# A graph-transformer layer on one core: the routing to the experts rebuilt, and weights split earlier

## The reference, cut to what matters

```python
xn = _layernorm(x)                                # x: 1250 x 1024, float32
x = x + gnn(xn, W, a, src, dst) + mix(xn, w_query_left, w_query_right, w_key, w_value)
x = x + ffn(_layernorm(x), gate_W, gate_b, expert_W, expert_b)

# gnn: h = xn @ W; e = exp(-leaky_relu(al[src] + ar[dst])) over 20000 edges;
#      elu(segment_sum(e * h[dst], src) / (segment_sum(e, src) + 1e-5))
# mix: ((xn @ w_ql) * (xn @ w_qr)) @ ((xn @ w_key).T @ (xn @ w_value))
# ffn: scores = maximum(x @ gate_W + gate_b, 1e-4); p = softmax(scores)      # 8 experts
#      the two largest of p are chosen; w = maximum(p, 0.1) / (sum of the chosen two)
#      out = sum over the chosen experts e of (x @ expert_W[e] + expert_b[e]) * w[e] / 2
```

## Time and profile before

| | us |
|---|---|
| median of 3 runs (1270.72 to 1272.55) | 1272.45 |
| the profiled execution, its own time | 1271.35 |
| its span | 1269.5 |
| PE busy in the span | 1190.3 (94%) |
| DVE busy | 760.4 (60%) |
| POOL busy | 486.7 (38%) |
| ACT busy | 305.9 (24%) |

### The profile page before, as it was taken

The page is one execution under the profiler, slowest core; times in us unless marked ns, Lnnn a source line. Parts: engine busy times, 40 slices in busy tenths (PEclk is TensorE's granted clock), DMA queues, the critical chain, the costliest instruction groups (busy, mean ns, idle before and its releaser), DMA issues.

```text
span 1269.5 us, 16268 instructions
## 1 busy us (share of the span) xinstructions
PE 1190.3 (94%) x5807; PEld 1002.7 (79%) x5807; DVE 760.4 (60%) x1525; ACT 305.9 (24%) x412; POOL 486.7 (38%) x446
## 2 busy tenths in 40 slices
PE   6999999999998999999999999899946799999996
PEld 5788888878787989899878878788744688878884
DVE  7979522453423777777663347989557933463544
ACT  2412112222110111211012323333243501331321
POOL 3940677878785000000000017455302444443443
PEclk9999999999998999999999999899957899999998
DMA  5110442834211233211054422333354974694844
GB/s 204 34 34 34 124 111 67 284 112 120 64 43 27 90 98 100 78 54 55 21 148 150 145 81 88 127 126 138 148 191 174 354 228 88 121 350 91 232 102 81
DMA packets 89623, 156.08 MB, mean 123 GB/s; under 512 B 14628, under 2 KB 45086, under 8 KB 89428
## 3 DMA queue, kind: packets, MB, share of 16 engines
q1 hardware_dynamic: 74148, 129.76, 29.7%
q0 software_dynamic: 15408, 25.44, 11.2%
HBM read 112.95 MB, written 42.04 MB: 122 GB/s over the span
## 4 chain that ended last, share of the span: by engine, by line
PE 57%; POOL 18%; DVE 15%; issue 8%; DMA 1%; ACT 1%; DVEq 0%; POOLq 0%; ACTq 0%
PE ps L1548 17%; PE ps L1549 17%; PE ps L1550 17%; POOL tab_d L650 16%; DVE e_lo L1463 3%; PE ps L1676 2%; PE ps L1738 2%; PE ps L1766 1%; DVE xn_lo L1017 1%; DVE stats L991 1%; PE ps L1635 1%; DMA e_raw<-in_L_ffn_expert_W 1%; DVE place_sum L1094 1%; DVE place L1092 1%; DVE place L1091 1%
## 5 line engine op out<-in xcount | busy, mean ns | idle before, releaser
L650 POOL DMA_INDIRECT tab_d<-val_i,addr_i x160 | 206.7, 1292 | 114.7 <-issue 114.7
L1548 PE MATMUL ps<-e_hi,lt_hi 128*128 128x512 f32 x368 | 147.8, 402 | 15.2 <-DVE lt_lo L1468 10.8
L668 POOL TENSOR_TENSOR att_part<-att 128x640 f32<-128x640 f32 x10 | 17.5, 1752 | 358.1 <-PE ps L1550 350.0
L1550 PE MATMUL ps<-e_hi,lt_lo 128*128 128x512 f32 x368 | 144.4, 392 | 0.0
L1549 PE MATMUL ps<-e_lo,lt_hi 128*128 128x512 f32 x368 | 144.2, 392 | 0.0
L1548 PE MATMUL ps<-xt_hi,q_hi 128*128 128x416 f32 (+1 forms) x384 | 143.4, 373 | 0.0
L1549 PE MATMUL ps<-xt_lo,q_hi 128*128 128x416 f32 (+1 forms) x384 | 136.2, 355 | 0.0
L1550 PE MATMUL ps<-xt_hi,q_lo 128*128 128x416 f32 (+1 forms) x384 | 135.7, 353 | 0.0
L1226 DVE TENSOR_TENSOR cnt<-ps,cnt 128x256 f32 x208 | 87.1, 419 | 42.3 <-PE ps L1676 28.1
L761 POOL DMA_INDIRECT out<-y,row_put x46 | 74.8, 1625 | 97.7 <-DVE y L1530 57.5
L1548 PEld LDWEIGHTS ps<-e_hi,lt_hi 128*128 128x128 f32 x368 | 69.6, 189 | 33.9 <-DVE yb L1525 14.6
(11 more groups left out here) (302 smaller groups left out, 2681.7 us busy)
## 6 DMA issues: line engine op xcount, KB each, us to landing
e_raw<-in_L_ffn_expert_W SPq DMA_DIRECT2D x64, 512.0 KB, 6.2
acc<-in_x SPq DMA_DIRECT2D x18, 512.0 KB, 8.9
w_raw<-in_L_mix_w_key SPq DMA_DIRECT2D x16, 512.0 KB
h_d<-hs SPq DMA_DIRECT2D x18, 256.0 KB
q_in<-q_d SPq DMA_DIRECT2D x9, 512.0 KB, 4.9
h_in<-h_d SPq DMA_DIRECT2D x9, 512.0 KB, 5.3
mix_d<-ms SPq DMA_DIRECT2D x18, 256.0 KB
mix_in<-mix_d SPq DMA_DIRECT2D x9, 512.0 KB, 3.2
```

Of the source, the lines that this page charges most:

```text
L650: nc.gpsimd.indirect_dma_start(out=tab_d, out_offset=bass.IndirectOffsetOnAxis(ap=addr_i[0:EP, j:j + 1], axis=0), in_=val_i[0:EP, j:j + 1] ...
L1548: nc.tensor.matmul(o, lh, rh, start=(k == 0), stop=False)
L1550: return nc.tensor.matmul(o, ll, rh, start=False, stop=(k == last_k))
```

## The change

The gaps "..." leave out declarations and index forms that only follow from what is shown.

1. Counting starts one PE job later, and DVE zeroes `cnt` in place of POOL.

```diff
+        TICK_FIRST = 3
         def tick_slots(j):
             per_job = 2
-            return range(min(NTK, per_job * max(0, j - 2)), min(NTK, per_job * max(0, j - 1)))
+            return range(min(NTK, per_job * max(0, j - TICK_FIRST)), min(NTK, per_job * max(0, j + 1 - TICK_FIRST)))
...
-            pool.wait_ge(s_wlo, UNITS * C_END)
-            pool.wait_ge(s_alsum, 1)
-            nc.gpsimd.memset(cnt[...].bitcast(f32), 0.0).then_inc(s_cz, 1)
...
             dve.wait_ge(s_alsum, 1)
+            V.memset(cnt[...].bitcast(f32), 0.0).then_inc(s_cz, 1)
             dve.wait_ge(s_tabr, 16)
```

```diff
+            for t in range(NT):
+                if t == NT - 1:
+                    rows_transposed(NT - 3)
...
+            nodes_half(NT - 1, 0)
+            weight_sums(NT - 1)
+            nodes_half(NT - 1, 1)
+            rows_transposed(NT - 2)
+            gate(NT - 4)
+            gate(NT - 3)
+            gate(NT - 2)
+            rows_transposed(NT - 1)
+            gate(NT - 1)
...
+                    pieces = [(NH - 1, slice(0, D))] if i < NT - 1 else [(h, slice(h * HALF, (h + 1) * HALF)) for h in range(NH)]
```

```diff
+                if t == 4:
+                    sp.wait_ge(s_full, first["GNN"])
+                    load_expert(0, range(MB))
+                if t == NT:
+                    sp.wait_ge(s_full, GNN_END)
+                    load_expert(0, range(MB, KB))
...
+            gate_in(NT - 3)
+            nodes_out(NT - 1)
+            act.wait_ge(s_full, GNN_END)
+            expert_hi(0, range(0, 1))
+            gate_in(NT - 2)
+            expert_hi(0, range(1, FIRST_LO))      # FIRST_LO = 3
+            gate_in(NT - 1)
+            expert_hi(0, range(FIRST_LO, KB))
             act.wait_ge(s_gate, 1)
             nc.scalar.activation(g_p[:, :, :], g_p[:, :, :], ACT.Exp).then_inc(s_gexp, 1)
...
+            expert_hi(1, range(FIRST_LO))
```

```diff
+            V.memset(sc[:, :, :], 0.0)
...
+            expert_lo(0, range(FIRST_LO))
+            dve.wait_ge(s_gate_used, NT)
...
+            V.tensor_reduce(g_tot[:, :], g_in[:, :, :], AX.X, ALU.add).then_inc(s_gtot, 1)
+            V.tensor_tensor(g_p[...], S, over_experts(g_m[:, :]), ALU.subtract).then_inc(s_gate, 1)
+            link(V.tensor_tensor_scan(g_run[...], flat2, flat2, 0.0, ALU.add, ALU.max))
+            link(V.tensor_copy(g_ends[:, 1:NE + 1], g_run[:, :, NT - 1]))
+            link(V.scalar_tensor_tensor(g_run[...], g_run[...], -1.0 - MID, over_ends(g_ends[:, 0:NE]), ALU.add, ALU.subtract))
+            dve.wait_ge(s_gtotp, 1)
+            link(V.tensor_scalar(g_nb[:, :], ps[:, 7, NE:2 * NE], 1.0 / P, MID / P, ALU.mult, ALU.add))
+            link(V.tensor_scalar(g_nb[:, :], g_nb[:, :], ROUND, None, ALU.add))
+            link(V.tensor_scalar(g_nb[:, :], g_nb[:, :], -ROUND, 1.0, ALU.add, ALU.max))
+            link(V.tensor_tensor_scan(g_cum[...], g_nb[...], g_nb[...], 0.0, ALU.add, ALU.max))
+            link(V.tensor_tensor(g_nb[:, :], g_cum[:, :], g_nb[:, :], ALU.subtract))
+            link(V.scalar_tensor_tensor(g_place[...], g_nb[...], float(P), ps[:, 7, 0:NE], ALU.mult, ALU.add))
+            V.tensor_tensor(g_pos[...], ...).then_inc(s_gpos, 1)
...
+            link(V.tensor_tensor(g_prod[:, :, :, :], g_pick[:, :, :, :], g_pos[...], ALU.mult))
+            link(V.tensor_reduce(p_f[:, :, :], g_prod[:, :, :, :], AX.X, ALU.add))
+            link(V.tensor_scalar(p_hi[...], p_f[...], 1.0 / P, ROUND, ALU.mult, ALU.add))
+            link(V.tensor_scalar(p_hi[...], p_hi[...], -ROUND, None, ALU.add))
+            link(V.scalar_tensor_tensor(p_lo[...], p_hi[...], -float(P), p_f[...], ALU.mult, ALU.add))
+            token_rows(0)                          # tok_r of the first choice, 128x1280
+            link(V.tensor_tensor(tok_s[...], ...))  # both choices, 128x580
+            for c in range(2):
+                last = V.tensor_tensor(tok_c[:, c * NT:(c + 1) * NT, :], ...)
+            last.then_inc(s_toks, 1)
+            token_rows(1).then_inc(s_toks, 1)
+            V.tensor_copy(bounds[:, 1:NE + 1], g_cum[:, :])
+            V.scalar_tensor_tensor(pad_0[...], g_nb[...], float(P), ps[:, 7, NE:2 * NE], ALU.mult, ALU.add)
+            dve.wait_ge(s_tokp, 1)
+            V.tensor_scalar(tok_of[:, :], ps[:, 2, 0:NSLOT], -1.0, 0.0, ALU.add, ALU.max).then_inc(s_route, 1)
+            V.tensor_scalar(slot_f[:, :], ps[:, 2, 0:NSLOT], -1.0, None, ALU.add)
```

```diff
-            gather(0)
+            gather_rows(tok_of[:, 0:1])
...
-            expert_lo(0, range(0, 1))
             block_lo(0, 0)
-            expert_lo(0, range(1, MB + 1))
+            expert_lo(0, range(FIRST_LO, MB + 1))
             block_lo(0, 1)
             expert_lo(0, range(MB + 1, KB))
...
+        AHEAD = [4] + [6] * (NE - 2)
             for e in range(NE):
                 if e + 1 < NE:
-                    expert_lo(e + 1)
+                    expert_lo(e + 1, range(AHEAD[e]))      # ACT: expert_hi(e + 1, range(0 if e else FIRST_LO, AHEAD[e]))
                 ... # the blocks of expert e
+                if e + 1 < NE:
+                    expert_lo(e + 1, range(AHEAD[e], KB))  # ACT: expert_hi(e + 1, range(AHEAD[e], KB))
...
                 if e >= 1:
                     sp.wait_ge(s_ye, first_block[e] * 2 + 2)
                     load_bias(e + 1)
+                if e + 2 < NE:
+                    load_expert(e + 2, range(KB), running=e)
```

More of the change, by code:

```diff
@@ L735, in _ @@
[L735 to L740 removed]
+            step(G.tensor_tensor(pad_at[:, :], pad_pre[:, :], pad_0[:, :], ALU.add))
@@ L1371, in _, with expert_lo @@
             dve.wait_ge(s_tri2, 3)
-            link(V.memset(sc[:, :, :], 0.0))
+            def expert_lo(e, rows):
+                for k in rows:
+                    dve.wait_ge(s_ehi, KB * e + k + 1)
+                    V.tensor_tensor(e_lo[e % 2][:, k, :], e_raw[k][:, :], e_hi[e % 2][:, k, :].bitcast(f32),
+                                    ALU.subtract).then_inc(s_elo, 1)
+            g_one, g_two = g_pick[:, 0], g_pick[:, 1]
+            V.memset(sc[:, :, :], 0.0)
+            V.memset(g_ends[:, :], 0.0)
+            V.memset(bounds[:, 0:1], 0)
+            V.tensor_scalar(io_mid[:, :], io16[:, :], -MID, None, ALU.add)
+            link(V.tensor_scalar(valid[:, :], tok[:, :], float(N), None, ALU.is_lt))
+            link(V.scalar_tensor_tensor(tokv[:, :], tok[:, :], 1.0, valid[:, :], ALU.add, ALU.mult))
+            expert_lo(0, range(FIRST_LO))
             dve.wait_ge(s_gate_used, NT)
@@ new lines, in gate @@
+            def gate(i):
+                w = ROWS[i]
+                if i == 0:
+                    pe.wait_ge(s_gw, 32)
+                    pe.wait_ge(s_cadd, NC)
+                pe.wait_ge(*released(tr_job[i] + 1))
+                for k in range(KB):
+                    last = nc.tensor.matmul(ps[0:w, 7, i * NE:(i + 1) * NE], xg[:, i % 2, k, 0:w], gw[:, k, :],
+                                            start=(k == 0), stop=(k == KB - 1))
+                last.then_inc(s_gate_used, 1)
@@ new lines, in rows_transposed, with nodes_half @@
+            def rows_transposed(i):
+                pe.wait_ge(s_xn2, NT + i + 1)
+                for g in range(2):
+                    n = tr_job[i] + g
+                    bank_free(n)
+                    transposes(n, xn2[:, i % 2, :], g, ROWS[i])
+            def nodes_half(t, h):
+                w, n = ROWS[t], gnn_half(t, h)
+                bank_free(n)
+                for d in range(NT):
+                    r = ROWS[d]
+                    last = three(ps[0:w, n % NB, :], att_hi[t % 2][0:r, d, 0:w], att_lo[t % 2][0:r, d, 0:w],
+                                 h_hi[0:r, d, h * HALF:(h + 1) * HALF], h_lo[0:r, d, h * HALF:(h + 1) * HALF], d, NT - 1)
+                last.then_inc(s_full, 1)
@@ new lines, in weight_sums @@
+            def weight_sums(t):
+                w, n = ROWS[t], gnn_sum(t)
+                bank_free(n)
+                pe.wait_ge(s_sum, t + 1)
+                nc.tensor.matmul(ps[0:w, n % NB, 0:2], att_sum[:, t % 2, 0:w], ones[:, 0:2], start=True, stop=True).then_inc(s_full, 1)
+            for t in range(NT):
+                if t == NT - 1:
+                    rows_transposed(NT - 3)
+                pe.wait_ge(s_attlo, t + 1)
+                if t == 0:
+                    pe.wait_ge(s_hlo, NT)
+                if t < NT - 1:
+                    for h in range(NH):
+                        nodes_half(t, h)
+                    weight_sums(t)
+                    if t >= 3:
+                        gate(t - 3)
+                    if t >= 2:
+                        rows_transposed(t - 2)
@@ L1780, in _ @@
             pe.wait_ge(s_pad, 1)
-            for c in range(2):
-                for e in range(NE):
-                    last = nc.tensor.matmul(ps[:, 6, 64:64 + NSLOT], pad_r[:, c, e, :], pad_c[:, c, e, :],
-                                            start=(c + e == 0), stop=(c == 1 and e == NE - 1))
+            for e in range(NE):
```

(1 more changed line is left out.)

342 lines of the change are left out of this document (143 added, 199 removed).

## The result

The changed kernel takes 1256.99 us (1250.6 to 1257.81, 4 runs), the kernel before 1272.5 beside it: ratio 0.987, 95% interval 0.9837 to 0.9904. It is faster, by 1.3%, and slower than the 1241 to 1254 that I gave. The profiled execution took 1256.91 (span 1255.1), 14.4 us under that of before, where 23.3 were forecast. Some 9 us are missing.

The account below looks back on a forecast made before the run. PE (94% busy) was taken as the bound, losing time waiting for DVE's chain, ACT's copies or DMAs. 1271.35 - 7.4 - 3.2 - 4.2 - 2.8 - 6.7 + 1.0 = 1248.05, so 1248 us; range 1241 to 1254.

Parts of the forecast that it names:

- Part 1: Counting at 402 us: starting one job later removes PE's 5.2 us stall and 2.2 of slow clock; -7.4 us.
- part 2: Last gates: reordered behind the GNN's last product, which ends 0.95 us later, they end at 934.0 instead of 937.14; -3.2 us.
- The new wait as a rival: Counting: DVE's memset delays POOL's scatters by 5.5 us, PE stalls about 4; 1254 us; chance 0.18, shared with late expert 2 tiles.
- Parts 2 to 4: Last gates -3.2, the chain to `tok_of` -4.2, from the route to the first expert block -2.8 us.
- more time at full speed: Gates: the clock stays up through them, -3.8 less 0.4 us; within 1241 to 1244; among faster variants, chance 0.27 together.
- The faster `tok_r`: Chain: `tok_r` runs at twice its pace with 16-bit operands, saving 2 x 0.75 us; 1246.5; among faster variants, chance 0.27 together.
- Part 5: Experts' first two blocks: fewer DVE splits ahead of `yb` cut PE's 8.85 us wait to about 4.5; -6.7, then +1 us.
- +1: Behind the second block: PE waits 1.4 us for expert 2's sixth tile, where it didn't before; +1 us.
- The rival of late tiles: Experts: expert 2's tiles come later, 4 us more and the slow start; 1254; chance 0.18, shared with the memset delaying scatters.
- Slower than before, by late tiles 6 and 7 in each block: Changes of expert: late loads stall PE 4 us plus 2.2 of slow clock, seven times; 1291 us; chance 0.03.

Follow-up runs that it names:

- e11: The changed kernel itself, unaltered, timed in more rounds and with a second profile; 1254.96 us (0.9876).
- e9: The changed kernel with the slow store of `al_d` issued right behind the first new loads of `q_in` and `kv_in`; 1255.32 us.
- e1: The kernel before with only the counting started one job later and DVE zeroing `cnt`; 1266.36 us (0.9949).
- e3: The changed kernel with the slow store of `al_d` issued four query steps later, ahead of a `kv_in` load; 1257.22 us (0.9908).
- e5: The changed kernel with only 512 of 1024 columns of each weight row loaded from expert 2 on; 1244.84 us (0.9787).
- e12: The kernel before with only 512 of 1024 columns of each weight row loaded from expert 2 on; 1270.65 us against 1271.81 (0.9992).
- e2: The changed kernel with counting from the second job and GpSimd zeroing `cnt` again, all else kept; 1262.37 us (0.993).
- e10: The changed kernel with `al_d`'s store behind the first loads, bounds read behind splits, four expert 0 tiles before the last gates, eight next-expert tiles ahead; 1245.49 us (0.9798).
- e6: The changed kernel with DVE's nine value_loads of bounds behind its splits of expert 1's first four tiles; 1250.6 us (0.9834).
- e4: The changed kernel with all eight tiles of the next expert split ahead of the present one's blocks, instead of six; 1253.49 us (0.9862).
- e7: The changed kernel with four instead of three tiles of expert 0 split by DVE ahead of the last gates; 1254.82 us (0.9877).

## Why the prediction was wrong, step by step

- **Part 1 (-7.4): right in kind, not reliable in size.** With the product's end put 0.95 later by part 2, H to product should be 6.45 shorter. It was 2.4 in the profiled run, 5.8 in e11, and 7.8 in e9, which has no late load at this place. Two terms were missing. I gave the memset's stall a margin of 0.7 us and didn't ask how much the scatters' end moves between executions: 8.7 us behind H in ten traces, 12.0 in two (the changed kernel and e1), 5.7 and 6.2 in two. Where it was 12.0, PE stood 1.9. And I named POOL's and DVE's queues but not SP's: without the stall, SP issues `q_in` directly behind `al_d`'s store. e3 and e9 show that term. In the profiled run `q_in` was used 9 us later than without it (13.3 for 4.2), in e11, where SP issued it 3.1 us behind the store, 6.5 later; e11 and e9 differ by 2 us from H to product.
- **The new wait as a rival (scatters held up by the memset):** the memset took 5.39 us on DVE and the scatters beside it kept their 1.19. Refuted.
- **Parts 2 to 4 (-10.2, and the 0.95): right.** Product to T is 11.35 shorter for 11.15 forecast. By step: 13.3 to the last gate (13.9), 13.8 to `tok_of` (13.7), 8.0 to the first `lt_lo` (7.9). Each was a sum of instruction lengths along one engine. Some traces have 2 us less, 33.0 instead of 35.0, where the clock fell later in the gates: from 3 to 6 us behind the product e9 has a granted clock of 1.00 and the changed kernel 0.58. I had given this more time at full speed as a rival and not in the sum.
- **The faster `tok_r`:** it took 1.50 and 1.48 us (1.49 before) with both operands of 16 bits. The rule of the Trainium skill that I set beside it (VectorE: DVE Perf Modes, section "Mode 2×_1P — pack two bf16 into one 32-bit read") asks for a step of 1 or -1. `p_lo`, repeated along the row, doesn't have it, and the trace agrees.
- **Part 5, up to the third block (-6.7, then +1): right.** PE idle 4.30 for 4.5. Behind the second block, where the "+1" was put for expert 2's tiles, it waited 0.74 (0.53 in e11) for 1.4; ACT took these six tiles 4.8 to 7.1 us behind their release, and I had put 7.9. The third block began at 33.3, 6.2 earlier than before, for 5.7 forecast.
- **Part 5, from the third block on: this is the step that failed.** "Later changes of expert still have eight splits between a block's end and the next `yb`, in another order: 0, with 0.5 either way for each of five." It was +7.2: of the 6.2 us that the third block was ahead, 3.5 went by the start of the fourth (a wait of 4.09 for 0.65) and 1.6 in the slow clock behind it, and 2.2 more at T+160 (3.13 for 0.96). T to end is +1.0 instead of -5.7. I counted DVE's splits and didn't ask when the tiles that they need would land. I had asked it for expert 2 alone, with the lag of one row of before (7.9 us). Expert 3's six came 10.0 to 13.8 us behind theirs, since the stream fills the DMA engines and needs 14 to 15 us for an expert (the estimate above), against 11.8 of block. e5 shows that it was the bytes: with half of them the sixth came 8.1 behind and the wait was gone. In the kernel before, 8.85 us of stall paid for the stream's delay (e12), so the earlier block gained nothing in the end while the loads started as they did.
- **The rival of late tiles** ("expert 2's tiles come later than by the 7.9 of before", 4 us more and the slow start, 1254) had the kind of wait and its size, but one change of expert too early: expert 2's tiles came in time, expert 3's didn't. Its part of the chance was small, and no rival named the changes behind it. That the time came out near its 1254 is luck.
- **Slower than before, by late tiles 6 and 7 in each block:** no such wait inside blocks in the two traces of the changed kernel, and 1.1 us in all at most in the others. But the order has a price at T+160 (3.13 to 4.88 with six tiles ahead and full loads, 1.20 and under 0.6 with eight), since the last two rows of expert 4 are released only behind expert 2's blocks, when expert 5's are due as well.
- **The 1.7 us ahead of H** are the clock's, and not the change's. H is 387.5 in the two traces without a low granted clock between 55 and 95 us (e2, e10). It is 388.9 to 389.0 in three with 3.4 us at 0.50 there (among them the changed kernel and e11), 390.5 to 390.8 in seven with 6.8 (among them the kernel before) and 392.2 to 392.6 in two with 10.2 (e9, e12).
- **What stays open:** why the scatters end 3 us sooner or later, and why the clock falls in that early stretch in one execution and not in another. Neither was tried. They are behind part of the spread from 1250.6 to 1257.8; how much isn't shown.

## What to carry to other kernels

When a stall is taken away, do the sum for each transfer stream that ran during it: its bytes over the rate that its own queue gets in the trace while the DMA engines are full, against the time of the work that it must keep up with. The rate of all queues together is too high for this (360 GB/s for 281 to 298 here). If the stream needs as long as the work or longer, the stall was its cover, and the wait comes back one or two steps on. Do the sum for every later change, not for the first alone. Look also at each in-order queue for what now comes directly behind a slow entry, and at every engine that must act before a transfer starts: in e6 the buffers were free, and SP was still reading its bounds.

## What the runs showed of the hardware

- The 5 KB store of `al_d` (1280 separate words) takes 9.2 to 12.6 us to land, and a load behind it on the same queue comes late, wherever it stands: issued 0.6 to 1.2 us behind it, `q_in` came 13.0 to 13.3 us behind its issue and `kv_in` 13.6 to 15.0, where some 4 and 5 are usual; issued 3.1 us behind it, `q_in` came after 10.6 to 10.9. A load issued 1.1 us ahead of the store was in time (3.8 and 4.2), and one issued 0.5 to 0.6 ahead took 6.4 to 7.2. The Trainium skill (DMA: Bandwidth & Descriptors, section "Queues, rings and completion order") says that each DMA engine takes descriptors in ring order; the traces of the loads behind the store agree.
- What a wait costs in clock differs with its length. From the first `yb` of expert 4's first block, behind which the wait at T+160 stands, to the next block's it took 7.1 to 7.2 us with waits of 0.96 to 3.13 (before, after, e1, e4, e11; granted clock behind it 1.00 in before and after), 8.7 to 8.8 with 3.5 to 4.0 (e2, e3, e6, e9; 0.72 in e9), and 9.9 with 4.88 (e7; 0.51). So a wait of 4 us cost 5.6 there, and one of 4.9 cost 7.6.
- DVE's sequencer reads nine bounds in 5.2 us. With nothing queued on the engine it stands idle for as long (5.19); with four splits queued ahead they run at the same time (e6).
- Half rows don't halve the engines' share: 0.93 and 0.78 at 258 and 209 GB/s in e5, for 1.03 and 1.04 at 362 and 357.
